# Head stacks in a fused cross-attention and expert kernel: another layout in DRAM, four stored copies, three on-chip pairs

## The reference, cut to what matters

```python
q = decoder_feature @ Wq.T          # decoder_feature = layernorm(x)
k = encoder_feature @ Wk.T          # encoder_feature = ctx_1024
q = q.reshape(b, t, 2 * HEADS, half).transpose(0, 2, 1, 3)   # 32 heads of half = 8 dims
k = k.reshape(b, n, 2 * HEADS, half).transpose(0, 2, 1, 3)
att = softmax(einsum('bhtd,bhnd->bhtn', q, k) * scale)
att = att.reshape(b, HEADS, 2, t, n)
att = att[:, :, 0] - lam * att[:, :, 1]
out = einsum('bhtn,bhnd->bhtd', att, v)
x = x + out
x = x + experts(layernorm(x))
```

## Time and profile before

| | |
|---|---|
| time, median of 3 runs | 2299.33 us (2287.5 to 2302.58) |
| span of the profiled execution | 2129.1 us |
| PE / DVE / ACT / POOL busy | 92% / 76% / 69% / 68% of the span |
| DMA | 606681 packets, 432.00 MB; 437572 packets under 512 B |
| mean granted TensorE clock | 0.968 of 2.4 GHz |

### The profile page before, as it was taken

One profiled execution on the slowest core, in us unless ns is written; L12 is line 12 of the kernel. 1 busy time (PEld: TensorE's weight loads), 2 busy tenths in 40 slices (PEclk: granted clock), 3 DMA queues, 4 the chain that ended last, 5 costly groups with the idle time before them and its releaser, 6 DMA issues.

```text
span 2129.1 us, 76257 instructions
## 1 busy us (share of the span) xinstructions
PE 1967.5 (92%) x20840; PEld 1418.7 (67%) x20840; DVE 1616.4 (76%) x4623; ACT 1464.5 (69%) x3511; POOL 1441.6 (68%) x2183
## 2 busy tenths in 40 slices
PE   3899999999999999999999999999989699999997
PEld 2555666666666666666666666666655599989996
DVE  2667788888778878888788887778776777767775
ACT  2567778777778777787787877777766455545554
POOL 4346677777677777677777777777656566656665
PEclk8799999999999999999999999999999799999999
DMA  4766676667666767666667676666774688868885
GB/s 122 195 189 194 186 199 189 203 203 199 190 185 196 204 189 196 194 195 194 198 194 201 190 200 193 192 190 191 212 211 161 206 266 263 259 200 274 256 267 172
DMA packets 606681, 432.00 MB, mean 203 GB/s; under 512 B 437572, under 2 KB 552395, under 8 KB 606161
## 3 DMA queue, kind: packets, MB, share of 16 engines
q1 hardware_dynamic: 546288, 319.87, 54.4%
q0 software_dynamic: 32256, 84.47, 10.9%
q10 hardware_dynamic: 28000, 26.03, 4.0%
HBM read 234.59 MB, written 197.72 MB: 203 GB/s over the span
## 4 chain that ended last, share of the span: by engine, by line
PE 54%; DMA 15%; SPq 14%; issue 7%; DVE 6%; POOL 3%; ACT 1%; DVEq 0%; POOLq 0%; ACTq 0%
DMA stacks<-mxT 8%; PE mx_ps L493 8%; SPq L369 7%; PE o_ps L526 6%; PE ms_ps L777 5%; PE ms_ps L554 5%; SPq L361 3%; SPq L354 3%; DMA stack_dram<-w_dn_sb 3%; PE mx_ps L554 3%; DMA stacks<-stack_dram 3%; PE mx_ps L556 3%; PE mx_ps L555 3%; PE ms_ps L555 3%; PE st_ps L755 3%
## 5 line engine op out<-in xcount | busy, mean ns | idle before, releaser
L981 DVE TENSOR_REDUCE mx<-mx_ps 128x4 f32<-128x512 f32 x1024 | 696.6, 686 | 234.4 <-PE mx_ps L493 229.7
L825 ACT ACTIVATE prob<-st_ps 128x512 f32<-128x512 f32 x1024 | 607.7, 596 | 318.4 <-PE st_ps L486 299.0
L493 PE MATMUL mx_ps<-stacks 48*128 48x128 bf16 x4096 | 397.7, 221 | 84.3 <-DMA stacks<-mxT 62.9
L486 PE MATMUL st_ps<-stacks 50*128 50x128 bf16 x4096 | 397.0, 221 | 0.0
L493 PEld LDWEIGHTS mx_ps<-stacks 48*128 48x128 bf16 x4096 | 232.4, 95 | 240.6 <-issue 130.5
L526 PE MATMUL o_ps<-prob,v_sb 128*32 128x256 f32 x4096 | 334.0, 398 | 0.9 <-ACT oT L812 0.6
L1343 POOL DMA_INDIRECT rows_dram<-rowt,posi x256 | 253.7, 991 | 67.9 <-issue 63.7
L554 PE MATMUL ms_ps<-e_lo 128*128 128x256 f32 x768 | 269.5, 351 | 18.6 <-DVE rowt L1080 9.8
L486 PEld LDWEIGHTS st_ps<-stacks 50*128 50x128 bf16 x4096 | 230.6, 95 | 2.6 <-issue 1.5
L555 PE MATMUL ms_ps<-e_lo 128*128 128x256 f32 x768 | 222.8, 290 | 0.0
L556 PE MATMUL ms_ps<-e_lo 128*128 128x256 f32 x768 | 221.8, 289 | 0.0
(11 more groups left out here) (155 smaller groups left out, 4667.3 us busy)
## 6 DMA issues: line engine op xcount, KB each, us to landing
stacks<-stack_dram SPq DMA_DIRECT2D x512, 192.0 KB
stack_dram<-w_dn_sb SPq DMA_DIRECT2D x192, 256.0 KB
stacks<-rows_dram SPq DMA_DIRECT2D x288, 130.0 KB
stack_dram<-w_dn_sb SPq DMA_DIRECT2D x64, 384.0 KB
stack_dram<-w_dn_sb SPq DMA_DIRECT2D x192, 128.0 KB
w_dn_sb<-in_x SPq DMA_DIRECT2D x64, 256.0 KB
w_dn_sb<-in_ctxT SPq DMA_DIRECT2D x64, 256.0 KB, 3.2
x_res<-in_x SPq DMA_DIRECT2D x64, 256.0 KB
```

The costliest lines, as they stand in the source:

```text
L486: return pe.matmul(st_ps[k % 2][:, i * P:(i + 1) * P], k_st[p][64 * h:64 * h + KROWS, u, j, :], q_st[p][64 * h:64 * h + KROWS, u, j, :], s ...
L493: return pe.matmul(mx_ps[k % 2][:, i * P:(i + 1) * P], q_st[p][64 * h:64 * h + ROWS, u, j, :], k_st[p][64 * h:64 * h + ROWS, u, j, :], sta ...
L825: nc.scalar.activation(prob[k % 4][:, :], st_ps[k % 2][:, :], ACT.Exp, scale=float(HALF) ** -0.5).then_inc(a_exp, 1)
L981: v.tensor_reduce(mx[:, u, c * CHUNK:(c + 1) * CHUNK], mx_ps[k % 2][:, :].rearrange("p (c n) -> p c n", c=CHUNK), AX.X, ALU.max).then_inc( ...
```

## The change

The dims (j t) of a row in DRAM take both sequences of the pair (`w` = 256 columns), so a row is 8 KB and the rows of a copy, and of neighbouring copies, lie one behind the other. Of the six copies four are stored, each by one put of 128 KB (eight puts a step instead of seven); the last two of the six are read from stored ones again. A load takes 32 rows (four copies) or 16 rows (two) of both sequences: eight loads a step, as before, of other shapes. The pairs of parts are the same six in another order. The loads of a step all stand behind the puts, the context's load and the next x; the maxima of b, `u` = 0, stand behind all eight loads. The residual's load stands ahead of the puts of k. A third pair of stacks lies in the experts' weights' place `e_hi`, free until the last steps; the semaphores of the loads are split by parity, so a put waits only for the loads of two steps before. With three stacks and two parities the loop takes six steps to an iteration instead of two (9 iterations instead of 27). POOL fills three k stacks with -1 at the start instead of two.

```diff
+COPIES = 4
+Q_COPIES, K_COPIES = (0, 1, 2, 0), (2, 0, 0, 1)
+Q_AGAIN, K_AGAIN = 0, 2
...
-    stack_dram = nc.dram_tensor("stack_dram", (2, 2, 2 * PARTS, 2, 2, HALF, SHH, P), BF16, kind="Internal").ap()
+    stack_dram = nc.dram_tensor("stack_dram", (2, 2, 2, COPIES, HALF, SHH, SW), BF16, kind="Internal").ap()
...
+        def stack_of_experts(n):
+            whole = e_hi[:, :, :, :].rearrange("p e k n -> p (e k n)").bitcast(BF16)
+            return whole[:, (2 + n) * SHH * SW:(3 + n) * SHH * SW].rearrange("p (j w) -> p j w", j=SHH)
+
+        q_st, k_st = [stack(2), stack_of_experts(0), stack(0)], [stack(3), stack_of_experts(1), stack(1)]
...
-        d_stk = [[sem(f"d_stk{u}{h}") for h in range(2)] for u in range(2)]
+        d_stk = [[sem(f"d_stk{i}{h}") for i in range(2)] for h in range(2)]
...
-            pipeline(eng, body, first, lo, hi, end, 2)
+            pipeline(eng, body, first, lo, hi, end, 6)
...
-                for u in range(2):
-                    for h in range(2):
-                        wait(sp, d_stk[u][h], STK, s, -STK)
-                for r, first, m in runs:
-                    sp.dma_start(stack_dram[s.par(), n, r:r + m].rearrange("r h u d j t -> (d j) (r h u) t"),
-                                 part[:, first:first + m, :].rearrange("p r (v t) -> p (r v) t", t=P)).then_inc(landed, 16)
-
-            def load_stacks(s, u, h):
-
-                p = s.par()
-                for n, buf in ((0, q_st[p]), (1, k_st[p])):
-                    sp.dma_start(buf[64 * h:64 * h + ROWS, u, :, :].rearrange("p j t -> p (j t)"),
-                                 stack_dram[p, n, :, h, u].rearrange("r d j t -> r d (j t)")).then_inc(d_stk[u][h], 16)
+                for h in range(2):
+                    wait_par(sp, d_stk[h], STK, s.plus(-2))
+                for i, r in enumerate(copies):
+                    sp.dma_start(stack_dram[s.par(), n, :, i].rearrange("h d j w -> (d j) h w"),
+                                 part[:, r, :].rearrange("p (h w) -> p h w", h=2)).then_inc(landed, 16)
+
+            def load_stacks(s, h):
+
+                p, i = s.par(), s.third()
+                for n, buf, again in ((0, q_st[i], Q_AGAIN), (1, k_st[i], K_AGAIN)):
+                    for row, copy, m in ((0, 0, COPIES), (COPIES * HALF, again, 2)):
+                        sp.dma_start(buf[64 * h + row:64 * h + row + m * HALF, :, :].rearrange("p j w -> p (j w)"),
+                                     stack_dram[p, n, h, copy:copy + m].rearrange("r d j w -> (r d) (j w)")).then_inc(
+                                         d_stk[h][p], 16)
...
-                if b.is_in(0, NS):
-                    wait(sp, p_st, NCH, it)
-                    wait(sp, p_mx, NCH, b)
-                    load_stacks(b, 1, 1)
-                    load_stacks(b, 1, 0)
                 if n2.is_in(0, NS):
                     wait(sp, g_qs, 1, n2, 1)
-                    put_parts(n2, 0, qp, d_qw, Q_RUNS[:1])
+                    put_parts(n2, 0, qp, d_qw, Q_COPIES)
                 if it.is_in(0, NS):
                     put_max(it, 1)
+                if b.is_in(0, NS):
+                    wait(sp, g_x2, 4, it, 0)
+                    sp.dma_start(x_res[1 - p][:, :, :], ...
                 if n2.is_in(0, NS):
-                    put_parts(n2, 0, qp, d_qw, Q_RUNS[1:])
                     wait(sp, g_ks, 1, n2, 1)
-                    put_parts(n2, 1, kp, d_kw, K_RUNS)
+                    put_parts(n2, 1, kp, d_kw, K_COPIES)
...
+                if n2.is_in(0, NS):
+                    wait(sp, p_st, NCH, it)
+                    wait(sp, p_mx, NCH, it)
+                    wait(sp, d_qw, PW_Q, n2, PW_Q)
+                    wait(sp, d_kw, PW_K, n2, PW_K)
+                    if n2.k is None and n2.off < 3:
+                        sp.wait_ge(g_ones, n2.off + 1)
+                    load_stacks(n2, 1)
+                    load_stacks(n2, 0)
+                if b.is_in(0, NS):
+                    put_max(b, 0)
...
-            for i in range(2):
-                g.memset(k_st[i][:, :, :, :], -1.0).then_inc(g_ones, 1)
+            for i in range(3):
+                g.memset(k_st[i][:, :, :], -1.0).then_inc(g_ones, 1)
```

More of the change, by code:

```diff
@@ L55, in par, with third @@
         return self.off % 2
+    def third(self):
+        return self.off % 3
     def pair(self):
@@ L269, in program @@
         first, lo, hi, end = -4, 4, NS - 6, NS + 3
+        assert (hi - lo) % 6 == 0 and (NS - 1) % 3 == 0
         PAD_STEPS = (*range(lo), *range(hi, hi + 4))
@@ L346, in _, with put_parts @@
                 sp.dma_start(lam_in[:, n, :], src.partition_broadcast(P)).then_inc(d_w, 16)
[L348 to L362 removed]
+            def put_parts(s, n, part, landed, copies):
+                for h in range(2):
[10 more added lines that the diff above has]
+                                         d_stk[h][p], 16)
             def put_max(s, u):
@@ L368, in put_max @@
                     row = 64 * h + ROWS
-                    sp.dma_start(q_st[s.par()][row:row + 2, u, :, :],
+                    sp.dma_start(q_st[s.third()][row:row + 2, :, u * P:(u + 1) * P],
                                  mxT[u][2 * SHH * h:2 * SHH * (h + 1), :]).then_inc(d_m[u], 16)
@@ L484, in scores @@
                 u, c = divmod(k, NCH // 2)
-                h, p, j = c // 4, s.par(), CHUNK * (c % 4) + i
-                return pe.matmul(st_ps[k % 2][:, i * P:(i + 1) * P], k_st[p][64 * h:64 * h + KROWS, u, j, :],
-                                 q_st[p][64 * h:64 * h + KROWS, u, j, :], start=True, stop=True)
+                h, p, j = c // 4, s.third(), CHUNK * (c % 4) + i
+                return pe.matmul(st_ps[k % 2][:, i * P:(i + 1) * P], k_st[p][64 * h:64 * h + KROWS, j, u * P:(u + 1) * P],
+                                 q_st[p][64 * h:64 * h + KROWS, j, u * P:(u + 1) * P], start=True, stop=True)
             def maxima(s, k, i):
                 u, c = divmod(k ^ 4, NCH // 2)
-                h, p, j = c // 4, s.par(), CHUNK * (c % 4) + i
-                return pe.matmul(mx_ps[k % 2][:, i * P:(i + 1) * P], q_st[p][64 * h:64 * h + ROWS, u, j, :],
-                                 k_st[p][64 * h:64 * h + ROWS, u, j, :], start=True, stop=True)
+                h, p, j = c // 4, s.third(), CHUNK * (c % 4) + i
+                return pe.matmul(mx_ps[k % 2][:, i * P:(i + 1) * P], q_st[p][64 * h:64 * h + ROWS, j, u * P:(u + 1) * P],
+                                 k_st[p][64 * h:64 * h + ROWS, j, u * P:(u + 1) * P], start=True, stop=True)
             def both(it, b, k, do_c, do_b):
@@ L499, in both @@
                 if do_b:
-                    if k % 4 == 0:
-                        wait(pe, d_stk[u][1 - k // 4 % 2], STK, b, STK)
+                    if k in (0, 4):
+                        wait_par(pe, d_stk[1 - k // 4], STK, b)
                     wait(pe, v_red, NCH, b, k - 1)
```

27 lines of the change are left out of this document (5 added, 22 removed).

## The result

The changed kernel takes 2678.09 us, median of 4 runs (2667.03 to 2683.33); the kernel before, on the same chip, 2296.4 us (4 runs, 2287.5 to 2302.58). The ratio is 1.1665, 95% interval 1.1618 to 1.1712: 382 us slower, where 41 us faster were forecast and the range ended at 2298.

A forecast was written before the change was run, and what follows sets the result against it. It took PE as bound by waits for the maxima's rows, with PE's own work close behind. Terms -62.9 (maxima) -5 (stacks) -15 (clock) +6 (DVE) +36 (branches) = -41 took 2299.3 to 2258 us; range 2210 to 2298.

The forecast's parts named there:

- The cause of the old wait: PE's 62.9 us wait for maxima rows came from SP's queue and loads on about six engines; it would go.
- DVE is next: DVE's small waits before PE, 7.8 us, would grow once PE waits less for DMAs: +6 us, bounds 0 and 15.
- SP waited 7.19 us for landed loads: SP's queue, after four stack loads, waits 7.19 us for their landing before the next put; this wait would go.
- The maxima of `u` = 0: Behind all eight loads, they land at T0 + 21.5 (T0: part k = 0); PE needs them at T0 + 23.3.
- rival 3: Slower: loads keep old issue time (2327 us) or six engines (over 2600); last-queued maxima land too late; chance 0.12.
- the term of -62.9 us: PE's whole wait for the landing of the maxima's rows, 62.9 us in the old profile, would vanish.
- the clock, put at -15: Of 19 us PE lost to the slow clock, most after waits, 15 come back; bounds 8 and 19.
- The 1.8 us of margin: SP's new circle, through puts, loads and maxima landing, would be some 1.8 us shorter than PE's own step.
- Loads at 282 GB/s: Stack loads spread over all 16 engines move 1.57 MB in 5.6 us; bounds 5.6 and 16.4 us.
- The puts of k, 3.8 us from the first issue to the last landing: Four puts of k in SP's queue, first at T0 + 10, all landed by T0 + 13.8.
- The branches back: Eight branches back of the six-step loop, 4.5 us each, cost 36 us; bounds 0 and 65.
- The signs that were named: Maxima wait under 10 us, none at k = 8; steps 23.3 to 23.6 us; wrong if PE waits at k = 0.

The follow-up runs named there:

- e2: Kernel before with only a DRAM layout where a load's 48 rows lie contiguous, each of six copies put by its own DMA: 2062.93 us, ratio 0.9639.
- e3: Kernel before without SP's wait for the loads' landing ahead of the puts: 2136.18 us, ratio 0.998.
- e14: Changed kernel with the residual's load moved behind the puts of k, run beside the changed kernel on one chip: 2516.53 us, ratio 1.1761.
- e9: Changed kernel with the maxima of b, `u` = 0, between the two halves' loads instead of behind them: 2274.51 us, ratio 1.0583.
- e10: Changed kernel with the maxima of `u` = 0 between the halves' loads and the residual's load behind the puts of k: 2212.23 us, ratio 1.0321.
- e1: Kernel before with only the loop changed, six steps to an iteration instead of two: 2221.85 us, ratio 1.0391.
- e15: Kernel before with contiguous 48-row loads, a put per copy, and six steps to an iteration instead of two: 2117.45 us, ratio 0.9893.
- e8: Kernel before in its old order, two stacks, two-step loop, but four stored copies and sixteen loads of 32 and 16 rows: 2273.1 us, ratio 0.988.

## Why the prediction was wrong, point by point

**The cause of the old wait: right in kind, half wrong in detail.** That the wait for the maxima came of loads on six engines, that it would go with them and that DVE is next, `e2` shows (62.9 to 3.8 us, DVE to 27.4 where 6 more were reckoned and 15 was the bound). That SP waited 7.19 us for landed loads, and that this was part of the circle, is wrong: `e3` finds 0.2%, inside the measurement, and the queue was issuing in that time. The third pair of stacks is not tied to that wait: it is there because a load of both sequences needs a stack that neither the scores of `it` nor the maxima of `it` + 1 still read. The place was misread too. The circle of the earlier trace rows ends at k = 0 in a wait of 0.33 us; some 50 of the 62.9 us stood at k = 8, in nearly each step, where the maxima of `u` = 1 come behind four loads and the big put:
```profile
824.75 0.21 PE L493 MATMUL mx_ps<-stacks 48*128 48x128 bf16 x1 [1.16 <-DMA stacks<-mxT]
...
849.31 0.21 PE L493 MATMUL mx_ps<-stacks 48*128 48x128 bf16 x1 [1.23 <-DMA stacks<-mxT]
```
That wait went, as forecast, in the changed kernel too. The new one is at k = 0, which was nearly free of waits: two loads stood ahead of the maxima of `u` = 0 in their part of the queue, and now eight do.

**"The maxima of `u` = 0": here the forecast failed.** The place was named as the dangerous spot, and rival 3 had the right mechanism. The step that failed is the landing of these maxima, put at T0 + 21.5 and measured at T0 + 30.8. So the term of -62.9 us became 328.8 - 62.9 = +266, and the clock, put at -15, cost 2.0 us of PE's work a step, some 128 us by estimate. The 1.8 us of margin were the difference of two sums, and four things made the longer one too short:

1. *The residual's load was not costed at all.* The prediction moved it in the text of the change and then took k's puts at T0 + 9.9, straight behind POOL's last part. SP's queue is in order, and the load waits for POOL's L1332, the last use of the old residual, done at T0 + 13.3. That held k's puts for 2.3 us a step, and its price is 59 us in all (`e14`).
2. *Loads at 282 GB/s.* That was 96 GB/s scaled by the share of engines. Where almost nothing but loads runs, 194 GB/s move at a share of 1.00, some 24 of them POOL's own DMAs; the loads' pieces lie between 821.5 and 830.5 us, 9.0 us for 1.57 MB instead of 5.6. The puts, which read all 128 partitions, do reach 260, so a busy share of 1.00 is not the engines' limit. The pieces of a load, 8 KB, take 0.73 us each (median in the loop), against 0.16 us for the 4 KB pieces of before, when six engines had the rows to themselves: more engines got a smaller rate each, as in `e2`. The Trainium skill (SBUF — State Buffer, "Door 1: The DMA port swizzle") says that partitions 0 to 63 reach only 8 of 16 ports, as do 0 to 31, 218 GB/s at most, and 64 to 127, where half 1 lies, the other 8. The trace agrees, with 194 in all; an estimate by the page's figure, while one half loads at a time, is 7.2 us or more for the loads. No run here moved the loads to other partitions, so that the ports are the cause is not shown.
3. *The puts of k, 3.8 us from the first issue to the last landing.* It was 5.3: four issues took 1.98 us instead of 1.4, and the last put landed 3.76 us after its issue, with the residual's 256 KB right ahead of the puts. Without that it was 4.7 (`e14`). The rate itself, 250 GB/s, was right, and so was the maxima's landing 1.1 us behind the loads' data, 1.3 by the trace; the 6.79 us from their issue are the loads' data ahead of them.
4. *The slow clock has a feedback.* The prediction took 15 us back from the clock. Once PE waits 5 us at k = 0, the next 4.8 us run at 0.52, the parts of k come 2.0 us later (2.6 in `e14`), and with them the puts, the loads and the maxima: PE's wait seems to lengthen its own cause. None of that stood in the circle. No run holds the clock and changes only the wait, so this share is read from one step each and not tried.

`e9` shows that the place decides: two DMAs put four loads earlier win back 301 of 434 us. With the residual's load out of the way too (`e10`) 366 are won back, and most of the rest stands at the branches.

**The branches back: right in kind, short in size.** 36 us were forecast with 0 and 65 as bounds; 82 in `e1`, 55 in `e15`. The idle time itself (4.0 each against 4.5) was well bounded by the landing of a DMA in those two kernels, not in the changed order of `e10`, where it is 6.9 each. What follows an idle time was put at nothing but the clock in it, and that was too little; which part of it is clock and which DMAs was not separated.

**The chances.** Rival 3 got 0.12 and "over 2600" was written beside it for loads on six engines. The loads kept all sixteen busy (issue 0.45 us each, 3.59 for eight, between the 0.36 taken and the 0.74 of the range), and the time came out there by other terms: that part is chance. A margin of 1.8 us in a circle of 23, made of rows read at other speeds, with an uncosted wait in it, was no 0.12.

**The signs that were named.** DMA share in the loop 0.58 and 133692 packets (0.55 and under 250000 forecast), instruction packets in the loop, L380 at 1.3 us for two, no wait at k = 8: all these came, and none of them is about time. Loads at over 200 GB/s did not come, nor steps of 23.3 to 23.6 us. The sign given for "wrong" came too, PE waits at k = 0 in each step.

**What remains of the loss when the causes are taken off.** On chips of one kind, the ratios go 1.201 (changed), 1.176 (residual later), 1.058 (maxima between the loads), 1.032 (both). The loop alone costs 1.039 in the kernel before and 1.027 in `e15`; divided out, as an estimate, 1.032 is 0.99 to 1.005, the kernel before. The four copies in the old order give 0.988, the 48 rows 0.963, but on chips of different kinds. So why eight 8 KB loads or four copies end some 2.5% behind the 48 rows was not tried piece by piece, and how much of it is the chip is open; in `e8` the wait for ACT's `v_sb` is the visible part (40 us, 1.7%).

## What to carry to other kernels

When small urgent transfers and large unhurried ones share a queue or the engines behind it, cost the small one from the end of the large one's data, not from its own size, and put it ahead; another queue alone does not save it. Before a DMA is moved in a queue, write beside it what it waits for and which instruction behind it is on the circle. When a chain of waits names a landing, look at whether the queue was issuing meanwhile, and read in the code what the wait asks for. And take the layout change alone first: here the rows of 48 one behind the other, with a put for each copy, gave the largest gain of any run, 3.6%; the longer loop that the third buffer forced cost 55 to 82 us by itself.

## What the runs showed of the hardware

- Where loads of 32 or 16 partitions fill all 16 engines, 194 GB/s move (24 of them not the loads'), with pieces of 8 KB that take 0.73 us; with puts from 128 partitions 260 GB/s at about the same share. A piece of 4 KB took 0.16 us in loads on six engines, 0.27 in loads of 48 partitions on sixteen.
- The issue of a load takes 0.45 us here, against 0.74 us in the kernel before, on six engines.
- A branch back to code no longer on chip stops PE for 3 to 5 us in `e1` and `e15`, 5.7 to 8.9 us in `e10`; eight of them cost 82 and 55 us in the first two.
- Two DMAs of 8 KB from ACT's queue landed 8.0 to 11.6 us after their issue beside eight loads of SP's.
- Chips differ: the part of the changed kernel behind the attention steps takes 506 us on one kind and 606 on the other, its steps 2034 and 2013; the kernel before takes 2140 and 2300 us. The cause was not looked for.
